# Attention on one core: float32 value products grouped by two and three key steps, over a ring of ten units of exponentials

## The reference

```python
scores = jnp.einsum('bqhd,bkhd->bhqk', q, k) / jnp.sqrt(jnp.float32(Dh))
attn = jax.nn.softmax(scores, axis=-1)
ao = jnp.einsum('bhqk,bkhd->bqhd', attn, v).reshape(B, S, D)
```

## Time and profile before

| what | value |
|---|---|
| median of 3 runs | 2101.25 us (2097.82 to 2107.39) |
| the profiled execution | 2100.15 us, of which 2098.3 us are the span |
| mean granted TensorE clock | 0.795 of full speed |
| busy share PE / DVE / ACT / POOL | 77% / 67% / 51% / 15% |
| `attention` of the first layer | about 996 to 1183 us of the span |
| `attention` of the last layer | about 1739 to 1922 us |

### The profile page before, as it was taken

How to read it: one execution, slowest core, us unless ns; L and a number is a source line. 1 busy time by engine, 2 the same in 40 slices (tenths; PEclk the granted TensorE clock), 3 DMA queues, 4 the chain that set the end, 5 groups by cost and what they waited for, 6 DMA issues and landing times. The chain is left out here.

```text
span 2098.3 us, 35935 instructions
## 1 busy us (share of the span) xinstructions
PE 1617.5 (77%) x13852; PEld 1161.0 (55%) x13852; DVE 1396.5 (67%) x3003; ACT 1069.7 (51%) x1862; POOL 305.6 (15%) x390
## 2 busy tenths in 40 slices
PE   5899965773999997759999840588517599998596
PEld 5888965763454455546444540588406463445375
DVE  6888965895544444464999467677465638995566
ACT  7989963234322221535699543555310245996265
POOL 0000000002533321012000010477400030000100
PEclk9999985875555556879799755799858797999698
DMA  4111010000000000100000034211110000000100
GB/s 123 35 46 32 2 31 12 4 1 0 1 1 1 1 0 6 29 9 1 1 2 2 4 101 137 69 55 56 52 53 0 2 8 1 2 2 4 29 1 31
DMA packets 44501, 49.87 MB, mean 24 GB/s; under 512 B 11000, under 2 KB 37334, under 8 KB 44332
## 3 DMA queue, kind: packets, MB, share of 16 engines
q1 hardware_dynamic: 38354, 32.67, 5.6%
q0 software_dynamic: 3840, 9.18, 1.5%
q10 hardware_dynamic: 2138, 5.72, 1.1%
HBM read 38.38 MB, written 9.19 MB: 23 GB/s over the span
## 5 line engine op out<-in xcount | busy, mean ns | idle before, releaser
L1869 DVE TENSOR_REDUCE att_max<-banks 104x1 f32<-104x512 f32 (+1 forms) x480 | 296.1, 684 | 16.0 <-PE banks L1784 11.9
L1904 ACT ACTIVATE att_p<-banks 104x514 f32<-104x514 f32 (+1 forms) x480 | 261.9, 599 | 33.1 <-PE banks L1827 22.4
L333 PE MATMUL banks<-tok_wT,feature_halves 128*128 128x192 f16 x2592 | 227.9, 248 | 23.5 <-DVE feature_halves L359 12.4
L333 PEld LDWEIGHTS banks<-tok_wT,feature_halves 128*128 128x128 f16 x2592 | 215.8, 99 | 32.5 <-DVE feature_halves L359 18.2
L1843 PE MATMUL banks<-att_p,att_v 104*32 104x257 f32 (+1 forms) x1920 | 159.3, 404 | 0.9 <-ACT att_p L1904 0.3
L1827 PE MATMUL banks<-att_q,att_kT 64*104 64x257 f16 (+1 forms) x960 | 156.0, 303 | 2.9 <-ACT att_p L1904 2.5
L1784 PE MATMUL banks<-att_kT,att_q 64*104 64x512 f16 (+1 forms) x480 | 128.0, 429 | 10.1 <-POOL att_last_keys L1754 8.0
L359 DVE TENSOR_TENSOR feature_halves<-features,feature_halves 128x2048 f16<-128x2048 f32 x54 | 123.4, 2285 | 5.4 <-ACT feature_halves L456 5.4
L1827 PEld LDWEIGHTS banks<-att_q,att_kT 64*104 64x104 f16 (+1 forms) x960 | 61.9, 123 | 106.3 <-ACT att_p L1904 79.8
L456 ACT CAST feature_halves<-features 128x2048 f16<-128x2048 f32 x54 | 102.2, 1893 | 9.8 <-PE banks L333 9.0
L1238 ACT CAST u_halves<-banks 57x384 f16<-57x384 f32 x36 | 17.0, 472 | 147.8 <-PE banks L1255 140.0
(11 more groups left out here) (460 smaller groups left out, 3691.1 us busy)
## 6 DMA issues: line engine op xcount, KB each, us to landing
tok_w<-in_L_tok_W_dram ACTq DMA_DIRECT2D x4, 1152.0 KB, 7.2
moe_w_in<-in_L_ffn_w_dram SPq DMA_DIRECT2D x8, 576.0 KB, 5.8
expert_y<-expert_out SPq DMA_DIRECT2D x6, 513.0 KB
moe_w_in<-in_L_ffn_w_dram SPq DMA_DIRECT2D x8, 384.0 KB, 3.6
moe_w_in<-in_L_ffn_w_dram SPq DMA_DIRECT2D x16, 192.0 KB, 4.6
raw<-in_x_dram SPq DMA_DIRECT2D x2, 1152.0 KB, 5.4
token_rows<-moe_rows SPq DMA_DIRECT2D x6, 342.0 KB
raw<-in_x_dram SPq DMA_DIRECT2D x2, 896.0 KB, 15.2
```

The lines of the kernel that those rows point to most:

```text
L333: ins = pe.matmul(c.bank[t // 2][:, (t % 2) * D:(t % 2 + 1) * D], fh[:, s, q, z, t * 128:(t + 1) * 128], wT[:, y, k, 6 * q + wf, :], start ...
L1869: dve.reduce_max(mx[0:qn, n // NS % 2, 2 * gi + e, k:k + 1], bank_of(unit)[0:qn, 0:ROW], X).then_inc(maxed, 1)
L1904: act.activation(p[0:kn, n % 4, :, :], c.pair[2 + n % 2][0:kn, :].rearrange("p (e q) -> p e q", e=2)[:, :, 0:HALF], ACT.Exp, scale=scale). ...
```

## The change

`values` is no longer called once for each step. With t the step of the main loop, nothing is called at most steps; at t with t % 5 = 2 the values of the first two key tiles of the current half are done in a row, and at t with t % 5 = 0 those of the three remaining ones. The order inside each call, the number of matmuls and the sums are the same. As exponentials have to be kept for longer, `p` gets ten units (five steps) in place of four, and ScalarE's wait for a free unit goes back by ten.

```diff
+    RING = 2 * NK
...
-        p = c.sb(ctx, name + "_p", [128, 4, 2, HALF])
+        p = c.sb(ctx, name + "_p", [128, RING, 2, HALF])
...
-                                        p[0:kn, (n + hh // 2) % 4, hh % 2, :],
+                                        p[0:kn, (n + hh // 2) % RING, hh % 2, :],
...
                         score_pair(LEAD + t)
                         keys(2 * t + 1)
-                    if t:
-                        values(2 * t - 2)
+                    for step in {2: (0, 1), 0: (2, 3, 4)}.get(t % NK, ()) if t else ():
+                        values(2 * ((t - 1) // NK * NK + step))
                     others(LEAD + t)
...
-                    if n >= 4:
-                        act.wait_ge(summed, (n - 4) // 2 + 1)
-                    act.activation(p[0:kn, n % 4, :, :],
+                    if n >= RING:
+                        act.wait_ge(summed, (n - RING) // 2 + 1)
+                    act.activation(p[0:kn, n % RING, :, :],
```

## The result

The changed kernel takes 2197.92 us (median of 6 runs, 2190.56 to 2202.31), the kernel before 2101.7 us in its 6 runs beside it. The ratio is 1.045, with a 95% interval of 1.042 to 1.048: 96 us slower, where 2171 us were forecast. That is 16 us above the range that went with the forecast itself (2160 to 2182), and inside the wide one (2138 to 2216). The profiled execution took 2201.53 us, 2199.7 of them the span; the mean granted clock is 0.775 in place of 0.795.

What follows compares the result with a forecast made beforehand. VectorE was taken to pace the main part, with TensorE close behind. 2100.15 + 50 (main part) + 17 (tails) + 4.5 (clock elsewhere) = 2171.6, forecast 2171 us; own range 2160 to 2182, wide range 2138 to 2216.

Steps and rivals of the forecast that it cites:

- VectorE as the pace, TensorE 0.05 us a step behind: Main part before the change: VectorE needs 1.20 us a step for two reductions, TensorE 1.15 us.
- So it adds nothing: Main part behind a block: ScalarE, run dry, takes 1.03 us a step, within VectorE's 1.20, so no added time.
- a chained call: Value call directly behind another on TensorE: 0.48 us taken, between 0.44 and 0.57, against 0.57 for a single call.
- V3: TensorE time of a block of three value calls at full clock: 1.53 us, bounds 1.45 and 1.71.
- V2: TensorE time of a block of two value calls at full clock: 1.05 us, bounds 1.01 and 1.14.
- VectorE's lateness V - 0.62: Main part: VectorE's wait for scores behind a block of length V, 0.91 us behind three calls, 0.43 behind two.
- The 50 us of the main part: Both layers' score waits, 28.1 us a layer less 3.2 us no longer waited: 24.9 a layer, 50 for two.
- The clock in the main part: One fifth of ten steps at half clock in each layer: 4.5 us, bounds 0 and 48 us.
- the clock falls in most groups: Main-part rival: half clock in most groups as well, 2171 + 44 = 2215 us; chance 0.15.
- The tails: Steps after the last scores, mostly at half clock: last layer 10.5 us more, first 6.3, together 17 us.
- The rules weighed: TensorE: mode changes drain it, agreeing with 0.13 us; bare same-row weight loads, 0.2 us or more a call, contradicted by trace.
- Faster: Rival: TensorE is the bound, score banks not drained, fewer mode changes save 26 us, 2075 us; chance 0.05.

Runs made afterwards that it cites:

- the square of experiments: Kernel before and changed kernel: nothing relieved 2101.7, 2197.9 us; halved reductions 2087.4, 2143.6; halved exponentials 2091.5, 2164.2; both halved 2074.5, 2100.1.
- The two kernels with doubled keys: Changed kernel, key matmuls issued twice in steps without a block and the last 13 steps: 2164.65 us; only in steps 8 and 9 of ten: 2161.55 us.
- the kernel with the ring alone: Changed kernel's ten units of exponentials, but values again called once each step; against the kernel before: 2101.14 us, ratio 1.000.

## Why the prediction was right, and where it was off

- VectorE as the pace, TensorE 0.05 us a step behind: right as a sum, and the group of 16.08 us against "near 16" came from it. So did VectorE's idle time of about 25 us a layer, 28 at full clock. Incomplete as a picture: the square of experiments shows the ScalarE loop 0.05 us a group behind VectorE in the kernel before, and as a floor of its own (15.38 us) in the changed one. "So it adds nothing" was right for the time and wrong as a remedy: who had mended only VectorE's wait would have got 0.7 of 2.4 us back.
- The cost of a block: a chained call is 0.43 to 0.44 us, the lower bound, where I took 0.48. V3 is 1.44 us (1.53 forecast), V2 1.00 us (1.05).
- VectorE's lateness V - 0.62: with the measured blocks it gives 0.82 and 0.38 us; 0.98 and 0.40 us were seen. The budget behind a block of three was 0.16 us too generous, and the two errors cancel (0.91 + 0.43 = 1.34 forecast, 1.38 seen), which is luck. That the waits would simply alternate was wrong: with last keys and turn in between they are 0.73 and 0.62 us of idle time. The 50 us of the main part came out as 52.
- The clock in the main part is the term that was mis-sized: 4.5 us forecast, 28 us in the profiled execution. I had seen that the stretch around the turn is thinner than anything before (it has two steps without values in a row, 8 and 9 of ten, not the three that I wrote), and even gave the bound for a fall in each group (48 us), but took one fall a layer as likely. 12 of the 20 groups behind the first of each layer had one. That is the condition of the rival "the clock falls in most groups" (0.15), at a smaller price than its 44 us, and a clock of 0.50 in the main part was named as a sign that the forecast is wrong: here it is. The two kernels with doubled keys show that this is the cause.
- Of the 30 us between the 2171.6 of the sum and the profiled 2201.5, 24 are that term. Another 5 lie ahead of the first attention, which is chance, and 2 in the first groups; main part (2 more) and tails (3 less) nearly cancel.
- The tails: five steps at half clock 9.95 us forecast, 1216.41 - 1206.53 = 9.88 seen; both at half clock, as said; 17 us forecast, 14 seen (18 against tails of 19.7 us, as the kernel with the ring alone has them).
- The rules weighed: the drain on a change of mode (the Trainium skill, "TensorEngine Tiling (Array Packing)", "Key Properties") is compatible with the 0.13 us that a chained call saves. That weight loads of the same rows would lie bare (the Trainium skill, "TensorE: Matmul & The Clock Gate", part 3) is not seen in a block of three: 24 records end with the next keys after 1.44 us, three times 0.44 and 0.12 for the change of mode.
- "Faster" (TensorE is the bound) had the right point of decision. What it needed, neither VectorE nor ScalarE as a pace, was built as far as halving their work does it, and even there grouping lost.

## What to carry to other kernels

Grouping like work on the engine that looks busiest pays only if what stands behind the group on its queue can wait: compare the length of the block with the work that the other engines have in store (here three banks of scores and two of keys), engine by engine, and expect more than one of them to run dry. Where two paces lie within a few hundredths of each other, relieving one buys next to nothing. And after evening out the sum, look at the thinnest stretch that the new order makes: if the clock can fall there, its price is paid on the long blocks that follow.

## What was not expected of the hardware

- Work for nothing made the kernel faster: eight extra matmul records a group (TensorE busy for 14.38 in place of 14.07 us of it) held the granted clock at 1.00 in the main part, and the kernel took 36 us less than 2198.
- Falls of the clock came in two sizes in the profiled execution: the disturbed groups took 17.5 to 17.7 us (nine) or 21.0 us (three), and none anything in between. In the long ones a stretch at 0.50 lasted through 12 us of the group, though TensorE was busy for 2.9 to 3.0 us of every 3 in it; ahead of the fall it had been busy for 2.62 and 2.53 of 3. The undisturbed group before it has 2.63 and 2.53 us in the same place (from 1832.90) and keeps its clock:

```profile
1849.00:1852.00 3.00, 2.62 (x34) 1.31 (x35) 2.37 (x6) 1.96 (x5) 0.00 (x0) 1.00 0.00 0
1852.00:1855.00 3.00, 2.53 (x21) 1.16 (x22) 2.93 (x6) 2.94 (x6) 0.00 (x0) 0.89 0.00 0
1855.00:1858.00 3.00, 3.00 (x28) 1.24 (x22) 0.76 (x2) 0.82 (x3) 0.00 (x0) 0.50 0.00 0
1858.00:1861.00 3.00, 2.92 (x22) 1.15 (x22) 2.48 (x4) 2.30 (x4) 0.00 (x0) 0.50 0.03 5
1861.00:1864.00 3.00, 2.92 (x21) 1.01 (x12) 1.29 (x3) 1.64 (x3) 0.00 (x0) 0.50 0.00 0
1864.00:1867.00 3.00, 3.00 (x25) 1.35 (x26) 2.39 (x4) 1.78 (x4) 0.00 (x0) 0.50 0.00 0
```

Why it stays low for so long in some groups and returns sooner in others was not tried and stays open.
